# At most two row scatters under way in the last four halves of a fused attention and expert kernel

## What is computed

```
x = x + _L0_xattn_ref(ctx_768, _layernorm(x, axis=-1), ...)     # 4 heads of 64; keys: 77 context rows and 1024 latents
x = x + _L0_ffn_ref(_layernorm(x, axis=-1), ...)
...
    pos = jnp.take_along_axis(jnp.cumsum(oh, 0) - 1, e[:, None], 1)[:, 0]
    valid = pos < CAP                                           # CAP = 256
    buf = jnp.zeros((E, CAP + 1, h), x.dtype).at[e, pos_c].set(x[token])[:, :CAP]
    g = jnp.einsum('ech,ehi->eci', buf, w_gate)
    u = jnp.einsum('ech,ehi->eci', buf, w_up)
    y = jnp.einsum('eci,eih->ech', jax.nn.silu(g) * u, w_down)
```

## Time and profile before

| what | value |
|---|---|
| time, median of 3 runs | 1085.38 us (1082.44 to 1087.95) |
| span of the profiled execution | 1168.4 us |
| PE busy | 906.8 us, 78% |
| DVE busy | 655.7 us, 56% |
| POOL busy | 581.3 us, 50% |
| ACT busy | 463.0 us, 40% |
| scatters (L1044) | 256, 251.2 us busy, 981 ns each |

### The profile page before, as it was taken

The page is one execution under the profiler, slowest core; times in us unless marked ns, Lnnn a source line. Parts: engine busy times, 40 slices in busy tenths (PEclk is TensorE's granted clock), DMA queues, the critical chain, the costliest instruction groups (busy, mean ns, idle before and its releaser), DMA issues.

```text
span 1168.4 us, 13234 instructions
## 1 busy us (share of the span) xinstructions
PE 906.8 (78%) x3848; PEld 626.7 (54%) x3848; DVE 655.7 (56%) x1956; ACT 463.0 (40%) x930; POOL 581.3 (50%) x522
## 2 busy tenths in 40 slices
PE   3869999999999999999964973957308999889300
PEld 2545666556656656656532542846207888777200
DVE  4475647875789775888652743743533443333206
ACT  3734675545755646664430521333103333222000
POOL 3530231204755635655665073155554888888850
PEclk9879999999999999999986995968658999999755
DMA  7739602012221422101261102000428999999689
GB/s 249 267 111 386 218 3 72 20 31 90 77 78 58 132 84 87 55 23 67 78 239 54 37 29 87 24 24 9 171 88 244 308 312 188 158 159 152 70 231 392
DMA packets 85335, 150.77 MB, mean 129 GB/s; under 512 B 14090, under 2 KB 53050, under 8 KB 83216
## 3 DMA queue, kind: packets, MB, share of 16 engines
q1 hardware_dynamic: 54543, 112.32, 27.8%
q0 software_dynamic: 30720, 37.61, 16.3%
HBM read 69.19 MB, written 97.45 MB: 143 GB/s over the span
## 4 chain that ended last, share of the span: by engine, by line
PE 48%; DVE 13%; issue 11%; POOL 8%; another core or an unknown queue 7%; DMA 7%; ACT 4%; POOLq 0%; SPq 0%; ACTq 0%; DVEq 0%
PE ps_o L1257 15%; PE ps_u L1154 6%; POOL sum L1111 4%; PE ps_s L1233 4%; PE ps_s L1235 4%; PE ps_u L1177 4%; DMA out_rows<-again,row_ids 3%; PE ps_u L1269 2%; PE ps_o L1252 2%; POOL out_rows L1111 2%; PE ps_u L1321 2%; DVE mp L1580 2%; PE ps_u L1165 2%; DMA sum<-again,row_ids 2%
## 5 line engine op out<-in xcount | busy, mean ns | idle before, releaser
L1044 POOL DMA_INDIRECT slot_rows<-rows,slot_idx x256 | 251.2, 981 | 312.0 <-issue 137.5
L1580 DVE TENSOR_REDUCE mp<-ps_u 128x1 f32<-128x512 f32 x256 | 165.1, 686 | 103.2 <-remote 49.6
L1450 ACT ACTIVATE probs<-ps_s 128x512 f32<-128x512 f32 x256 | 139.9, 596 | 176.6 <-PE ps_s L1235 105.4
L1111 POOL DMA_INDIRECT sum<-again,row_ids x84 | 130.0, 1548 | 26.5 <-issue 22.6
L1257 PE MATMUL ps_o<-probs,pool 128*128 128x512 f32 (+1 forms) x288 | 138.0, 602 | 2.5 <-ACT den L1471 2.5
L1321 PE MATMUL ps_u<-again 128*128 128x256 f32 x512 | 123.9, 386 | 0.0
L1257 PE MATMUL ps_o<-probs,V 128*128 128x512 f32 (+1 forms) x216 | 106.4, 615 | 10.4 <-ACT probs L1453 5.9
L1235 PE MATMUL ps_s<-qbT,Kb 65*128 65x512 f32 (+1 forms) x252 | 102.4, 406 | 0.0
L1752 DVE TENSOR_SCALAR again<-ps_o,again 128x256 f32<-128x256 f32 x128 | 56.1, 480 | 82.3 <-DMA sum<-again,row_ids 54.7
L1154 PE MATMUL ps_u<-wqkv_s,lnT 128*128 128x512 f32 (+1 forms) x256 | 97.4, 515 | 4.1 <-ACT lnT L1373 3.2
L1321 PEld LDWEIGHTS ps_u<-again 128*128 128x128 f32 x512 | 94.2, 194 | 11.0 <-issue 0.3
(11 more groups left out here) (190 smaller groups left out, 1610.8 us busy)
## 6 DMA issues: line engine op xcount, KB each, us to landing
again<-in_wexp SPq DMA_DIRECT2D x64, 384.0 KB, 5.3
slot_rows<-rows SPq DMA_DIRECT2D x2, 10272.0 KB, 35.0
again<-slot_rows SPq DMA_DIRECT2D x64, 321.0 KB
sum<-rows SPq DMA_DIRECT2D x2, 4352.0 KB, 27.6
again<-sum SPq DMA_DIRECT2D x8, 1024.0 KB, 11.3
Kb<-K SPq DMA_DIRECT2D x16, 275.5 KB
pool<-in_x SPq DMA_DIRECT2D x4, 1024.0 KB, 5.5
xres<-in_x SPq DMA_DIRECT2D x8, 512.0 KB
```

The lines of the kernel that those rows point to most:

```text
L1044: pool.indirect_dma_start(out=slot_rows, out_offset=bass.IndirectOffsetOnAxis(ap=slot_idx[x][:, q, k:k + 1], axis=0), in_=rows[x][:, q, :] ...
L1111: pool.indirect_dma_start(out=(out, *sums)[e % PLANES], out_offset=bass.IndirectOffsetOnAxis(ap=row_ids[:, e % RING, t:t + 1], axis=0), in ...
L1450: act.activation(probs[:, n % NPR, hh, :], ps_s[:, u % NSC, :], ACT.Exp).then_inc(s["probs_made"], 1)
L1580: v.tensor_reduce(mp[:, i, tile, half:half + 1], bank((*t, i))[:, :], AX.X, ALU.max).then_inc(s["emptied_vec"], 1)
```

## The change

In the last four halves scatter number n of a half waits, from the third on, until scatter n-2 has landed. For that, even and odd scatters of an x get a semaphore each, and all other waits for a half's scatters wait for both. Each engine's instructions stay in the same order.

```diff
-HALF_SCATTERS = 16 * QT * TOPK
+HALF_SCATTERS = 16 * QT * TOPK // 2
...
-                 "slots_made", "rows_made", "scattered0", "scattered1",
+                 "slots_made", "rows_made", "scattered00", "scattered01", "scattered10", "scattered11",
...
             for x in range(2):
-                sp.wait_ge(s[f"scattered{x}"], B * HALF_SCATTERS)
+                for n in range(2):
+                    sp.wait_ge(s[f"scattered{x}{n}"], B * HALF_SCATTERS)
...
                 if plan.paced(b, x, q, k) and k % 2 == 0:
                     pool.wait_ge(s["values_done"], plan.paced(b, x, q, k) + 1)
+                if plan.paced(b, x, q, k) is None and TOPK * q + k >= 2:
+                    pool.wait_ge(s[f"scattered{x}{k % 2}"], HALF_SCATTERS * b + 16 * ((TOPK * q + k) // 2))
                 pool.indirect_dma_start(
                     out=slot_rows, out_offset=bass.IndirectOffsetOnAxis(ap=slot_idx[x][:, q, k:k + 1], axis=0),
                     in_=rows[x][:, q, :], in_offset=None, bounds_check=E * CAP - 1,
-                    oob_is_err=False).then_inc(s[f"scattered{x}"], 16)
+                    oob_is_err=False).then_inc(s[f"scattered{x}{k % 2}"], 16)
...
-                            act.wait_ge(s[f"scattered{x}"], HALF_SCATTERS * b)
+                            for n in range(2):
+                                act.wait_ge(s[f"scattered{x}{n}"], HALF_SCATTERS * b)
...
-                        v.wait_ge(s[f"scattered{x}"], HALF_SCATTERS * b)
+                        for n in range(2):
+                            v.wait_ge(s[f"scattered{x}{n}"], HALF_SCATTERS * b)
```

## The result

The changed kernel takes 1118.07 us (median of 4 runs, 1115.12 to 1119.41), the kernel before on the same chip 1085.29 us (1082.44 to 1087.95). The ratio is 1.0298, 95% interval 1.0273 to 1.0323: slower by 3%, 33 us. Forecast were 1091 us and a range up to 1098. The profiled execution of the changed kernel took 1119.41 us and has a span of 1117.7.

A forecast was written before the change was run, and what follows sets the result against it. PE was taken as the bound in ordinary attention, with only POOL's last 32 scatters able to move the end. Semaphore split 0, earlier halves 0 and about 6 us there, added to 1085.4, gave about 1091 us, range 1074 to 1098.

The forecast's parts named there:

- the reading of the 83 us between span and times: Whole trace: profiled execution 83 us longer than timed runs, so most of the stall belongs to profiling; timed runs hardly have it.
- What hides it: Halves before the last: POOL about 12 us later, hidden by its 18.4 us addition wait and 38.5 us idle; cost 0.
- My sum: Last 32 scatters, in the trace's time: loss 4.4 to 6.1 us if routing tables are ready as late as there.
- POOL alone as the bound: Rival (c), last 32 scatters: without DVE lateness POOL bounds the end, loss 12 to 14 us, 1098 to 1099; chance 0.08.
- the pause of 1.66 us: Near the end of each 32 scatters, one start comes 1.66 us later than usual, without a releaser the profile shows.
- The quiet pair of 2.92 us: Limited scatters in quiet: landing 2.09 plus restart 0.83 us per pair, 1.46 per scatter, 0.18 more than before.
- Beside loads I had 5.0 us: Limited scatters beside weight loads: a pair takes 4.5 to 5.5 us, mean 5.0, instead of 2.56.
- The restart of 0.83 us: POOL from a wait's release to the scatter's start: 0.83 us taken, with 0.30 as lower bound.
- the landing: Scatter beside the 17 weight loads of the last half: landed 3.7 to 4.7 us after its start.
- The cost of 0 for the split of the semaphores: Consumers at ACT, DVE and SP wait on two semaphores instead of one: cost 0, uncovered below 1 us in all.
- (b): Rival, 600 to 820 us: thinning the series relieves any stall in timed runs, 1072 to 1076 if 15 to 20 go; chance 0.22.

The follow-up runs named there:

- three-memset kernel: Kernel before with split semaphores, no limit, three 128x1 memsets ahead of each of the 120 scatters; 1086.45 us beside 1086.07, 1146.6 beside 1161.2 on a stalling chip.
- e8: Changed kernel with the limit only in three of the last four halves and only even k waiting; 1096.57 us beside 1086.07 of the kernel before.
- e10: Changed kernel with even-k waits in three halves, four under way in the first 16 scatters beside the 16 weight loads; 1087.47 us beside before's 1086.07.
- split kernel: Changed kernel without the wait on scatter n-2, two semaphores kept; 1160.66 us beside before's 1161.73, again 1174.84 beside 1169.23.
- the last kernel: Even-k waits in three halves, four under way in the first 16 scatters beside the 16 weight loads; on a stalling chip 1095.11 us beside before's 1161.2.

## Why the prediction was wrong

**What failed first** is the reading of the 83 us between span and times: "I take it that most of this stall belongs to the profiled execution". The stall is in the timed executions too, on some chips. Wherever both were taken of one execution, span and time agree to 2 us (1117.7 and 1119.41; 1158.8 and 1160.53). The guess was right in its use, that the timed comparison had no stall, and wrong in its cause.

**What failed next, and cost the most,** is the step "What hides it". It laid POOL's delay in the first three halves under POOL's idle time of 18.66 and 38.5 us. That idle time was the stall's own work: PE and DVE were late, so POOL had nothing to do. The same holds for the addition that waited 18.4 us for its rows. Having put the stall aside for the timed runs, I should have taken its idle time away too. The three-memset kernel's trace without a stall shows the real cover; the addition follows its scatters at once there, at 633.65 us (POOL's timeline at the first scatters of the parts, and the last one):

```profile
643.95 0.99 POOL L1050 DMA_INDIRECT slot_rows<-rows,slot_idx  x1 [7.30 <-issue]
...
699.61 0.97 POOL L1050 DMA_INDIRECT slot_rows<-rows,slot_idx  x1 [13.41 <-issue]
...
726.70 0.99 POOL L1050 DMA_INDIRECT slot_rows<-rows,slot_idx  x1 [0.62 <-issue]
...
789.44 0.97 POOL L1050 DMA_INDIRECT slot_rows<-rows,slot_idx  x1 [0.16 <-issue]
```

The cover is 7.3 us before 643.95, 13.4 before 699.61 and 3.4 before 726.70 (0.62 in the line, 2.74 ahead of its memsets), 24 us in all, and from there on none: 48 scatters follow without any idle time but the gaps of the series, to 789.44. In the changed kernel POOL needed 65.4 us from the first to the last of the 32 scatters that start at about 591 us, where this one needs 41.5: 24 us, against the 12 I had for that half and part of the next. The next half cost 13.6 us more (54.8 against 41.2), the third 5.5 (2.1 us longer, and without the 3.4 us of cover in its midst). These 43 us used up the cover of 24, and the last half began 18.8 us late (766.91 against 748.15). That is the failed step with its number: a cost put at 0, at most 12 us, measured at 18.8.

**The last 32 scatters.** From 766.91 to 823.81 us they take 56.9 us, in the other kernel 748.15 to 789.44, 41.3: 15.6 us. My sum had 4.4 to 6.1 under a late DVE chain and 12.3 to 14 with POOL alone as the bound. The second was the case, which I had made a rival with a chance of 0.08; it too was short, partly because the pause of 1.66 us, which I took for a part of every series, isn't there without the stall: the unlimited last halves of e8 to e10 take 39.7 to 40.0 us, so the loss is nearer 17 us by them. 18.8 + 15.6 = 34.4 us, and the first row load comes 34.4 us later (826.08 against 791.70), within 2 us of the 32.8 us measured.

**Sizes.** The quiet pair of 2.92 us was right (2.8 us). Beside loads I had 5.0 us; 5.9 and 7.25 were measured at the first loads, and 6.6, 6.4 and 5.4 from 774.12 us on, beside the 17. The restart of 0.83 us was right, 0.76 to 1.07 were measured; the landing was mis-sized, 5.15 and 6.17 us at the first loads and 5.8, 5.5 and 4.6 beside the 17, where I had 3.7 to 4.7. The cost of 0 for the split of the semaphores stands, by the three-memset kernel's 1086.45 beside 1086.07.

**The rivals.** That the stall could be relieved, (b), was right as a mechanism and wrong in its place: on chips that stall the change wins 50 us (0.9555). It asked how much of the stall the timed runs have; that this would differ by the chip no rival had. That the change came out slower, as forecast, rests on the chip of the comparison and was luck in that much.

**Open** is how the stall comes about and why only some chips have it. Shown is where it lies (unbroken series of scatters 1.28 us apart), that waits which really hold POOL take it away, that four under way or 1.32 us don't, and that rare breaks do so in part. Whether it is the holding that counts or the mean distance isn't shown, as the waits thin the series too: on stalling chips the 32 scatters of the second of the four halves take 40.0 us in the split kernel, 46.6 with every fourth waiting, where part of the stall is left, and 50.9 and 55.9 in the last kernel and the changed one, where the long waits are gone.

## What to carry to other kernels

Before cover (idle time of an engine that may hide a delay) is taken from a trace, ask what made the idle time: if it is the stall that is being removed or set aside, it is no cover. When a profiled span and the timed runs differ by more than a few us, find out whether they come from the same kind of chip before explaining the gap. A limit on transfers under way is paid where their landing is long, beside other traffic; there it should be wider (9 us here), and in the last part, with nothing behind it, absent, unless the stall that it removes lies there too.

## What the runs showed of the hardware

One kernel, two times: 1085 to 1086 us on two chips, 1161 to 1169 us on three. The difference lies in stretches in which POOL issues indirect DMAs without a break; there ACT and DVE wait up to 20.5 us without a releaser, though the DMA engines are nearly idle in one of them (share 0.09). Not all of such a wait is lateness, as PE itself may be late with the operand. Two pairs of before's timeline show how much is: DVE's row maximum starts 9.7 us after the end of its matmul, the only thing that the code has it wait for (613.85 to 623.56), and ACT's copy of a block's output 15.4 us after the end of the block's last value matmuls (701.49 to 716.92).

```profile
613.05 0.80 PE L1177 MATMUL ps_u<-K,Q 128*128 128x512 f32 x1 [7.64 <-DVE mp L1580]
...
623.56 0.69 DVE L1580 TENSOR_REDUCE mp<-ps_u 128x1 f32<-128x512 f32 x1 [9.83 <-remote]
...
699.42 2.07 PE L1257 MATMUL ps_o<-probs,V 77*128 77x512 f32 x2 [1.39 <-ACT probs L1453]
...
716.92 0.59 ACT L1470 ACTIVATE oT<-ps_o 64x512 f32<-64x512 f32 x1 [17.55 <-remote]
```

The expert phase's series of adding DMAs in the same trace, 1.85 us apart (1040.66 and 1042.51 us), shows none of it. And a 128x1 memset of 0.11 us between two scatters moves nothing: it fits into their 0.30 us, and the time stays that of the split kernel on that chip (1175.91 and 1174.84).
